# Cross-attention and gated expert attention on one core: turned x tiles by DMA, a reordered prologue, and the last batch's projection in pieces

## The chip, the core and the metric

One core of a Trainium2 chip runs the whole program. The metric is the device time of one launch in microseconds (us); lower is better.

## The reference, cut to what matters

`x` is 8 batches of 512 rows of 512 values, `ctx` 8 batches of 77 rows.

```python
x = x + (softmax(mask(layernorm(x) @ ctx.T * scale)) @ ctx).swap(-1, -2) @ W_merge.T + b_merge   # per batch
h = layernorm(x)                                                # taken as 4 x 1024 rows
rw = softmax(relu-gated cosine logits of h against sim, 16 experts)
q, k, v = [sum_e rw[e] * (h @ proj[e]) for proj in (q_proj, k_proj, v_proj)]    # head width 64
a = softmax(causal(q @ k.T / 8)) @ v
x = x + sum_e rw[e] * (a @ o_proj[e])
```

Gating and attention work on whole rows. Products are made in three parts of a high and a low half of each operand (`products`), so each expert product is 12 matmuls.

## The kernel before

Rows are taken in tiles of 128; a batch is 4 tiles. The program is written by hand for each engine: one instruction stream for TensorE (PE), VectorE (DVE), ScalarE (ACT), GpSimd (POOL) and SyncE (SP), joined by semaphores. Every engine works strictly in the order of its stream, and SP issues every DMA, all on one queue.

After a prologue, a batch is 32 slots, `k` from 0 to 31; slot `k` is expert pair `g = k % 8` of tile `j = k // 8`. In each slot TensorE makes 12 expert matmuls into one of four banks `psQ` (400 columns for `g` = 0, 384 otherwise). Around them the body places the other work of the kernel by slot, from tables at the head of the file:

- **Cross attention, five tiles ahead** (`X1_LEAD`). At `g` = 0 (`X1_T_SLOT`) TensorE turns the x tile in `H` with four transposes into `psT`, and ScalarE and VectorE copy it to the pair `hT` (`copy_rows`, `low_rows`). `x1_score` follows at `g` = 4, its softmax after it (`x1_limit`, `x1_exp`, `x1_invert`, `x1_high`, `x1_low`).
- **The next tile's h.** `sum_x2` and `add_x2` at `g` = 2, its row statistics, GpSimd's `powers`, `normalise` at `g` = 4, and at `g` = 6 four transposes of `H` (`move_rows`).
- **The causal attention of the batch**, from slot 15 on: turned q and k (`QK_T_AT`), scores into `psM` (`SCORES_AT`), reciprocal and scaling, turned probabilities (`PROBS_T_AT`), values into `psM` (`VALUES_AT`).
- **The output projection.** For each half of the batch (two tiles) and each of four groups `u` of experts: `MIX_AT` multiplies `spread` (the gates, repeated over partitions by a DMA) with the attention, `MIX_LO_AT` makes its low part, `PROJECT_AT` makes 12 matmuls of 512 columns, six into `psO` and six into `psM`. `Y_AT` adds the residual.

Slots over 31 in a table lie in the next batch. For the last batch there is no next one: slots 32 to 48 are a body without expert products.

The prologue takes the first five tiles through cross attention, makes the first merged matrix `G`, the normalised `sim`, the first h, and starts on the high and low parts of the expert weights (`w_high`, `w_low`, 8 pieces of 128x1536), which go on into the first slots. ScalarE and VectorE also make the parts of `w_o` in slots 9 to 23.

## Time and profile before

| | |
|---|---|
| median of 3 runs | 931.87 us (930.38 to 932.78) |
| profiled execution | 931.5 us, its span 929.8 us |
| busy: PE, weight loads, DVE, ACT, POOL | 894.8, 834.4, 646.0, 224.3, 126.0 us |
| mean granted TensorE clock | 0.982 |
| DMA | 88.60 MB, 95 GB/s over the span |

The profile has one execution's instructions with start and duration. Matmuls overlap, so their durations add up to more than the time; the distance between two starts tells what one costs. A bracket behind a row is the idle time of the engine before it, and who ended it.

### The profile page before, as it was taken

What the parts mean: (1) busy time and instruction counts of PE and PEld (TensorE: products, weight loads), DVE (VectorE), ACT (ScalarE), POOL (GpSimd) and SP (SyncE); (2) the same over time, 40 slices, a digit from 0 to 9 for tenths busy, and PEclk for the clock granted to TensorE, in tenths of its full rate; (3) what the DMA queues carried; (4) which work ended last, traced back from release to release, by engine and by line L of the source; (5) the groups of instructions that cost most, each with busy time, mean ns of one, the idle gap of its engine ahead of it and who ended that gap; (6) DMA issues with size and microseconds to landing.
All of it is one profiled execution on the core that took longest, in us unless ns stands there. A gap on an engine that the chain in (4) does not pass through costs nothing.

```text
span 929.8 us, 16166 instructions
## 1 busy us (share of the span) xinstructions
PE 894.8 (96%) x5000; PEld 834.4 (90%) x5000; DVE 646.0 (69%) x1964; ACT 224.3 (24%) x570; POOL 126.0 (14%) x333
## 2 busy tenths in 40 slices
PE   6679999999999999999999999999999999999976
PEld 5579999999999899999999999999999999999965
DVE  6788877767586776767777676776758676666643
ACT  4522312213131221212212131211312121121121
POOL 3221111201111110111111011110101211110100
PEclk9699999999999999999999999999999999999997
DMA  8912513144141531334113441414314251132131
GB/s 265 342 54 77 171 38 83 60 113 134 49 116 38 135 104 48 104 86 152 47 60 93 94 153 37 113 40 119 129 45 107 64 145 38 50 91 69 35 72 42
DMA packets 63493, 88.60 MB, mean 95 GB/s; under 512 B 10297, under 2 KB 33497, under 8 KB 63170
## 3 DMA queue, kind: packets, MB, share of 16 engines
q1 hardware_dynamic: 63426, 87.84, 32.3%
q8 instruction: 25, 0.41, 0.2%
q14 instruction: 42, 0.34, 0.1%
HBM read 68.68 MB, written 19.14 MB: 94 GB/s over the span
## 4 chain that ended last, share of the span: by engine, by line
PE 79%; DVE 7%; issue 6%; DMA 4%; SPq 1%; DVEq 1%; ACT 1%; POOLq 1%; POOL 1%; ACTq 0%
PE psQ L1212 47%; PE psO L1305 10%; PE psM L1305 9%; PE psT L1130 3%; DMA MASK<-in_mask 2%; PE psT L1162 2%; PE psO L1153 2%; PE psM L1280 2%; DMA merge_lo<-merge_scratch 1%; PE psT L1145 1%; DVE neg_mx L1043 1%; PE psT L1147 1%; DVE acc L919 1%; PE psT L1239 1%; PE psT L1220 1%
## 5 line engine op out<-in xcount | busy, mean ns | idle before, releaser
L1212 PE MATMUL psQ<-Wqkv_hi,hT_hi 128*128 128x384 f32 (+1 forms) x1024 | 352.6, 344 | 4.7 <-DVE hT_lo L795 2.9
L1212 PE MATMUL psQ<-Wqkv_lo,hT_hi 128*128 128x384 f32 (+1 forms) x1024 | 347.6, 339 | 0.0
L1212 PE MATMUL psQ<-Wqkv_hi,hT_lo 128*128 128x384 f32 (+1 forms) x1024 | 347.6, 339 | 0.0
L919 DVE SCALAR_TENSOR_TENSOR acc<-psQ,RW,acc 128x192 f32<-128x192 f32 x448 | 165.0, 411 | 130.9 <-PE psQ L1212 128.6
L1212 PEld LDWEIGHTS psQ<-Wqkv_hi,hT_hi 128*128 128x128 f32 x1024 | 193.3, 189 | 11.1 <-DVE hT_lo L795 3.3
L1212 PEld LDWEIGHTS psQ<-Wqkv_lo,hT_hi 128*128 128x128 f32 x1024 | 193.4, 189 | 4.7
L1212 PEld LDWEIGHTS psQ<-Wqkv_hi,hT_lo 128*128 128x128 f32 x1024 | 193.4, 189 | 0.0
L551 POOL TENSOR_TENSOR pow_tmp<-b_mv,eps 128x1 f32<-128x1 f32 x32 | 7.5, 234 | 682.0 <-DVE b_mv L872 682.0
L755 ACT ACTIVATE mixedT_hi<-spread 128x512 fp32r<-128x512 f32 x64 | 40.5, 632 | 203.6 <-DVE spread L1095 148.2
L619 ACT ACTIVATE hT_hi<-psT 128x512 fp32r<-128x512 f32 x64 | 38.0, 595 | 134.5 <-PE psT L1130 134.5
L1305 PE MATMUL psO<-Wo_hi,mixedT_hi 128*128 128x512 f32 x128 | 55.1, 431 | 2.7 <-DVE mixedT_lo L1086 2.7
L795 DVE TENSOR_TENSOR hT_lo<-psT,hT_hi 128x512 fp32r<-128x512 f32 x64 | 44.0, 688 | 15.3 <-ACT hT_hi L619 14.6
L1305 PE MATMUL psO<-Wo_hi,mixedT_lo 128*128 128x512 f32 x128 | 50.8, 397 | 0.0
L1305 PE MATMUL psO<-Wo_lo,mixedT_hi 128*128 128x512 f32 x128 | 50.6, 395 | 0.0
L1305 PE MATMUL psM<-Wo_lo,mixedT_hi 128*128 128x512 f32 x128 | 50.4, 394 | 0.0
L1305 PE MATMUL psM<-Wo_hi,mixedT_lo 128*128 128x512 f32 x128 | 50.4, 394 | 0.0
L1305 PE MATMUL psM<-Wo_hi,mixedT_hi 128*128 128x512 f32 x128 | 50.3, 393 | 0.0
L1086 DVE TENSOR_TENSOR mixedT_lo<-spread,mixedT_hi 128x512 fp32r<-128x512 f32 x64 | 43.5, 680 | 7.0 <-ACT mixedT_hi L755 6.0
L1095 DVE TENSOR_TENSOR spread<-spread,attT 128x512 f32<-128x512 f32 x64 | 43.5, 680 | 3.5 <-ACT attT L766 3.5
L738 ACT ACTIVATE qkT<-psT 128x256 fp32r<-128x256 f32 x32 | 12.3, 384 | 139.4 <-PE psT L1239 139.4
L1130 PE MATMUL psT<-ident,H 128*128 128x128 f32 x236 | 36.1, 276 | 3.9 <-DVE H L876 2.9
L881 DVE SCALAR_TENSOR_TENSOR logit<-psQ,pow_out,neg_sig 128x16 f32<-128x16 f32 x32 | 7.5, 234 | 43.8 <-PE psQ L1212 43.8
(178 smaller groups left out, 1283.5 us busy)
## 6 DMA issues: line engine op xcount, KB each, us to landing
spread<-gates_scratch SPq DMA_DIRECT2D x32, 512.0 KB, 6.6
X<-in_x SPq DMA_DIRECT2D x32, 256.0 KB, 2.7
x_scratch<-X SPq DMA_DIRECT2D x32, 256.0 KB, 2.0
resid<-x_scratch SPq DMA_DIRECT2D x32, 256.0 KB, 4.1
out<-resid SPq DMA_DIRECT2D x32, 256.0 KB, 2.4
merge_hi<-merge_scratch SPq DMA_DIRECT2D x28, 256.0 KB, 2.9
merge_lo<-merge_scratch SPq DMA_DIRECT2D x28, 256.0 KB, 3.3
H<-in_x SPq DMA_DIRECT2D x27, 256.0 KB, 2.9
```

The lines of the kernel that those rows point to most:

```text
L619: act.activation(hT[p][0][:], psT[moves.bank()][:], ACT.Copy).then_inc(moved_hi, 1)
L755: act.activation(mixedT[0][:, 2 * (u % 2):2 * (u % 2) + 2, :], spread[:, 2 * u:2 * u + 2, :], ACT.Copy).then_inc(mix_hi, 1)
L795: dve.tensor_tensor(dst, src, dst_hi.bitcast(F32), ALU.subtract).then_inc(moved_lo, 1)
L919: dve.scalar_tensor_tensor(out=acc[e][:], in0=src, scalar=w, in1=acc[e][:], op0=ALU.mult, op1=ALU.add).then_inc(expert_added, 1)
L1086: dve.tensor_tensor(mixedT[1][:, 2 * (u % 2):2 * (u % 2) + 2, :], spread[:, 2 * u:2 * u + 2, :], mixedT[0][:, 2 * (u % 2):2 * (u % 2) + 2, ...
L1095: dve.tensor_tensor(pair_of, pair_of, attT[:].unsqueeze(1).broadcast_to([P, 2, 2 * P]), ALU.mult).then_inc(mix_made, 1)
L1130: last = pe.transpose(bank[:, c * P:(c + 1) * P], tile[:, c * P:(c + 1) * P], ident[:])
L1153: last = pe.matmul(psO[0:CP, :], a[:, q, :], w, start=(q == 0 and n == 0), stop=(q == TILES - 1 and n == 2))
L1162: last = pe.matmul(bank[:], a[:], w[:], start=(n == 0), stop=(n == 2))
L1212: last = pe.matmul(psQ[g % 4][:, 0:first_col(g) + PW], a[:, c * P:(c + 1) * P], w[:, c, E + g * PW - first_col(g):E + (g + 1) * PW], start ...
L1280: last = pe.matmul(psM[:, cols], v[:, s, :, :].rearrange("p r d -> p (r d)"), w[:, s * 2 * P:s * 2 * P + cols.stop], start=(m == 0), stop= ...
L1305: last = pe.matmul((psO, psM)[i][:], a[:, 2 * (u % 2) + c, place(i)], w[:, 2 * u + c, :], start=(u == 0 and c == 0 and n == 0), stop=(u == ...
```

## The change

The host gives the kernel a second copy of x, `x_t`, in which each 128x512 tile is already turned.

1. **Turned tiles.** The four transposes at `g` = 0 go. SP loads the turned tile into `XT` at the tile's first slot (`load_xt`), ScalarE and VectorE make `hT` of it at `g` = 2 (`turned_high`, `turned_low`).
2. **Prologue.** ScalarE issues the first four turned tiles on its own DMA queue. The first two expert weight pieces are issued earlier, `w_o` in slots 5 and 11. The squares of `sim` and the bias' low part move to GpSimd, the 128x16 power there comes before the fifth tile. The fifth tile's scores and softmax move to slots 3 and 4. The low parts of weight pieces 0 and 1 are made in halves, between which the first h is worked on.
3. **Last batch.** Tiles 2 and 3 are turned at slots 26 and 32, scored at 28 and 33. The first half's projection is in pieces in slots 31 to 37, the second half's in 38 to 41, in banks of its own (`psQ` 2 and 3); the last scores and values use `psQ` 0 and 1. The gates of the last half come in four loads.

```diff
 QK_T_AT = ({15: 0, 18: 1, 31: 2, 34: 3},
-           {15: 0, 18: 1, 31: 2, 34: 3})
+           {15: 0, 18: 1, 26: 2, 32: 3})
 SCORES_AT = ({18: 0, 20: 1, 34: 2, 36: 3},
-             {18: 0, 20: 1, 34: 2, 36: 3})
+             {18: 0, 20: 1, 28: 2, 33: 3})
 INVERT_AT = ({19: 0, 21: 1, 35: 2, 37: 3},
-            {19: 0, 21: 1, 35: 2, 37: 3})
-PROBS_T_AT = ({21: 0, 23: 1, 37: 2, 39: 3},) * 2
-SCALE_AT = ({20: 0, 22: 1, 36: 2, 38: 3},) * 2
+            {19: 0, 21: 1, 29: 2, 34: 3})
...
 SPREAD_SLOT = 16
 SPREAD_1_SLOT = 3
-VALUES_AT = ({25: 0, 41: 1},) * 2
+LAST_SPREAD_AT = {31: (0, 1), 34: (2,), 36: (3,)}
+VALUES_AT = ({25: 0, 41: 1}, {25: 0, 35: 1})
 MIX_AT = ({26: (0, 0), 27: (0, 1), 28: (0, 2), 29: (0, 3),
            42: (1, 0), 43: (1, 1), 44: (1, 2), 45: (1, 3)},
-          {26: (0, 0), 27: (0, 1), 28: (0, 2), 29: (0, 3),
-           42: (1, 0), 43: (1, 1), 44: (1, 2), 45: (1, 3)})
+          {26: (0, 0), 27: (0, 1), 32: (0, 2), 34: (0, 3),
+            36: (1, 0), 37: (1, 1), 38: (1, 2), 39: (1, 3)})
 MIX_LO_AT = tuple({k + 1: job for k, job in at.items()} for at in MIX_AT)
-PROJECT_AT = tuple({k + 2: job + ((0, 1),) for k, job in at.items()} for at in MIX_AT)
+PROJECT_AT = ({k + 2: job + ((0, 1),) for k, job in MIX_AT[0].items()},
+              {31: (0, 0, (0,)), 32: (0, 0, (1,)), 33: (0, 1, (0, 1)), 34: (0, 2, (0,)), 35: (0, 2, (1,)),
+                36: (0, 3, (0,)), 37: (0, 3, (1,)), 38: (1, 0, (0, 1)), 39: (1, 1, (0, 1)), 40: (1, 2, (0, 1)),
+                41: (1, 3, (0, 1))})
+STORE_Y_AT = ({31: 0, 33: 1, 47: 2, 48: 3}, {38: 0, 39: 1, 47: 2, 48: 3})
 Y_AT = ({31: 0, 32: 1, 47: 2, 48: 3},
-        {31: 0, 32: 1, 47: 2, 48: 3})
+        {38: 0, 39: 1, 41: 2, 42: 3})
...
-X1_T_SLOT, X1_MOMENTS_SLOT, X1_SCORE_SLOT, X1_INV_SLOT, X1_LOW_SLOT = 0, 3, 4, 5, 6
+X1_HIGH_SLOT, X1_MOMENTS_SLOT, X1_SCORE_SLOT, X1_INV_SLOT, X1_LOW_SLOT = 2, 3, 4, 5, 6
...
+SCORE_4_SLOT, ATT_4_SLOT = 3, 4
 WO_AT = {9 + 2 * n: n for n in range(8)}
+WO_LOAD_AT = {5: 0, 11: 1}
+RESID_SLOT = 25
...
+        def project_banks(h, ab):
+
+            return (psQ[2], psQ[3]) if h == 1 and last_batch(ab) else (psO, psM)
...
+                def load_xt(t, p):
+
+                    if isinstance(t, int) and t == 0:
+                        sp.wait_ge(x1_max_ready, TILES)
+                    else:
+                        sp.wait_ge(qkv_summed, PAIRS * t)
+                    sp.dma_start(XT[p][:], turned(t + X1_LEAD)).then_inc(xt_in, 16)
...
+                load_w(0)
+                sp.dma_start(xt_first[TILES], turned(TILES)).then_inc(ld_xt[TILES], 16)
...
+                load_w(1)
...
+                        if cross and g == 0 and not (is_first(b) and j == 0):
+                            load_xt(t, (j + 1) % 2)
...
+                    if n == 1:
+                        pool.wait_ge(ld_sim, 16)
+                        pool.tensor_tensor(sim_sq, sim_f, sim_f, ALU.mult).then_inc(sim_squared, 1)
+                        pool.wait_ge(bias_made, 1)
+                        pool.tensor_tensor(bias_lo, bias_f, bias_hi.bitcast(F32), ALU.subtract).then_inc(bias_made, 1)
+                pool.wait_ge(sim_floored, 1)
+                pool.tensor_tensor(sim_rn, sim_ss, half_e, ALU.pow).then_inc(sim_rooted, 1)
...
+                act.dma_start(xt_first[0], turned(0)).then_inc(ld_xt[0], 16)
                 act.wait_ge(ld_ctx[0], 16)
                 centre(ctx_first[0], centre_dump, 0)
+                for n in range(1, TILES):
+                    act.dma_start(xt_first[n], turned(n)).then_inc(ld_xt[n], 16)
                 act.wait_ge(dve_init, 1)
                 copy_ctx()
-                copy_rows(0)
-                copy_rows(1)
+                turned_high(0, 0)
+                turned_high(1, 1)
                 act.wait_ge(ld_bias, 16)
...
+                def turned_low(t1, p):
+
+                    dve.wait_ge(xt_hi, t1 + 1)
+                    src = xt_first[t1] if isinstance(t1, int) and t1 < X1_LEAD else XT[p][:]
+                    high, low = x1_parts[t1] if isinstance(t1, int) and t1 < X1_LEAD else hT[p]
+                    dve.tensor_tensor(low[:, 0:D], src, high[:, 0:D].bitcast(F32), ALU.subtract).then_inc(xt_lo, 1)
...
+                    chunks = slice(0, KC) if half is None else slice(half * KC // 2, (half + 1) * KC // 2)
+                    last = dve.tensor_tensor(Wv[1][:, chunks, cols], W_raw[:, chunks, cols],
+                                             Wv[0][:, chunks, cols].bitcast(F32), ALU.subtract)
+                    if half != 0:
+                        last.then_inc(w_lo, 1)
...
-                G_low(0)
-                dve.wait_ge(gate_e_made, 1)
-                link(dve.tensor_scalar(gate_e, gate_e, 1.0, None, ALU.add))
-                link(dve.reciprocal(gate_e, gate_e))
-                dve.tensor_scalar(neg_sig[:], gate_e, -1.0, None, ALU.mult).then_inc(const_ready, 1)
-                x2_moved = add_x2(None)
-                dve.wait_ge(sim_summed, 1)
-                dve.tensor_scalar(sim_ss, psM[:, 0:E], NORM_FLOOR ** 2, None, ALU.max).then_inc(sim_floored, 1)
-                row_stats(x2_moved)
-                low_ctx()
-                w_low(0)
+                turned_low(TILES, 0)
...
                 last.then_inc(sim_normed, 1)
+                dve.wait_ge(gate_e_made, 1)
+                link(dve.tensor_scalar(gate_e, gate_e, 1.0, None, ALU.add))
+                link(dve.reciprocal(gate_e, gate_e))
+                link(dve.tensor_scalar(neg_sig[:], gate_e, -1.0, None, ALU.mult))
+                G_low(0)
+                w_low(0, 0)
+                x2_moved = add_x2(None)
+                row_stats(x2_moved)
+                dve.wait_ge(sim_hi, 1)
+                dve.tensor_tensor(simn[1], sim_f, simn[0].bitcast(F32), ALU.subtract).then_inc(sim_lo, 1)
+                w_low(0, 1)
+                normalise(0, 0)
+                low_ctx()
+                w_low(1, 0)
                 low_rows(0)
-                normalise(0, 0)
-                x1_limit(TILES, 0)
-                dve.wait_ge(sim_hi, 1)
-                dve.tensor_tensor(simn[1], sim_f, simn[0].bitcast(F32), ALU.subtract).then_inc(const_ready, 1)
-                w_low(1)
-                low_rows(0)
+                w_low(1, 1)
                 w_low(2)
-                x1_invert(TILES, 0)
-                x1_low(TILES, 0, 0)
...
-                        if cross and g == X1_T_SLOT:
-                            move_rows(H, x1_in, 32 * (t + 1))
-                            x1_moved = moves.now()
+                        if qkv and is_first(b) and k == SCORE_4_SLOT:
+                            x1_score(TILES, 0)
...
+                                if h == 0 and last_batch(ab):
+                                    pe.wait_ge(exp_done, TILES * ab + 3)
...
         "x": _np.asarray(x),
+        "x_t": _np.asarray(x).reshape(-1, 128, D // 128, 128).transpose(0, 3, 2, 1).reshape(-1, D),
```

TensorE in the middle of batch 0, first before, then after (`H` is the x tile, `psQ` takes the expert products):

```order
L1212 MATMUL psQ<-Wqkv_lo,hT_hi 128x400
L1212 MATMUL psQ<-Wqkv_hi,hT_lo 128x400
L1130 MATMUL psT<-ident,H 128x128 x4
L1212 MATMUL psQ<-Wqkv_hi,hT_hi 128x384
L1212 MATMUL psQ<-Wqkv_lo,hT_hi 128x384
```
```order
L1302 MATMUL psQ<-Wqkv_hi,hT_hi 128x400
L1302 MATMUL psQ<-Wqkv_lo,hT_hi 128x400
L1302 MATMUL psQ<-Wqkv_hi,hT_lo 128x400
L1302 MATMUL psQ<-Wqkv_hi,hT_hi 128x384
L1302 MATMUL psQ<-Wqkv_lo,hT_hi 128x384
```

The transposes between the 400-column and the 384-column products are gone.

VectorE in the prologue, before from the first x2 sum on, after from the low part of `G` on (`H` is the first normalised tile, the last `hT_lo` in each the turned form of a tile, `spread` the space in which `sim` is prepared):

```order
L865 TENSOR_TENSOR X<-psT,X 128x512
L972 TENSOR_SCALAR spread<-psM 128x16
L870 BN_STATS b_stats<-X 128x6
L872 BN_AGGR b_mv<-b_stats 128x2
L795 TENSOR_TENSOR ctxT<-psT,ctxT 128x2x77 x2
L848 TENSOR_TENSOR Wqkv_lo<-W_raw,Wqkv_hi 128x4x384
L978 TENSOR_TENSOR spread<-spread 128x16 x4
L795 TENSOR_TENSOR hT_lo<-psT,hT_hi 128x512
L876 TENSOR_SCALAR H<-X,b_mv,pow_out 128x512
L819 COPY sc<-psT 128x77
L821 TENSOR_TENSOR sc<-psT,sc 128x77
L825 SCALAR_TENSOR_TENSOR sc<-sc,x_scale,limit 128x77
```
```order
L951 TENSOR_TENSOR G_lo<-psO,G_hi 77x512
L939 TENSOR_TENSOR Wqkv_lo<-W_raw,Wqkv_hi 128x2x384
L958 TENSOR_TENSOR X<-psT,X 128x512
L963 BN_STATS b_stats<-X 128x6
L965 BN_AGGR b_mv<-b_stats 128x2
L1070 TENSOR_TENSOR Wqkv_lo<-spread,Wqkv_hi 128x4x16
L939 TENSOR_TENSOR Wqkv_lo<-W_raw,Wqkv_hi 128x2x384
L969 TENSOR_SCALAR H<-X,b_mv,pow_out 128x512
L878 TENSOR_TENSOR ctxT<-psT,ctxT 128x2x77 x2
L939 TENSOR_TENSOR Wqkv_lo<-W_raw,Wqkv_hi 128x2x384
L878 TENSOR_TENSOR hT_lo<-psT,hT_hi 128x512
L939 TENSOR_TENSOR Wqkv_lo<-W_raw,Wqkv_hi 128x2x384
```

Half of a weight piece stands where the wait for the sum is, the other half after the statistics; the first h no longer has a whole piece and the fifth tile's low part ahead of it, and its own `hT_lo` follows after half a piece.

TensorE after the last expert product, before:

```order
L1239 MATMUL psT<-ident,nat 128x128 x2
L1261 MATMUL psM<-qkT 128x384
L1262 MATMUL psM<-causal_r,ident_r 128x128
L1264 MATMUL psM<-kT_lo,qkT 128x384
L1261 MATMUL psM<-qkT 128x512
L1262 MATMUL psM<-causal_r,ident_r 128x128
L1264 MATMUL psM<-kT_lo,qkT 128x512
L1220 MATMUL psT<-ident,probs 128x128 x7
L1280 MATMUL psM<-probsT_hi,V_hi 128x256
```

After, around the last scores, and around the last turned probabilities:

```order
L1403 MATMUL psM<-Wo_lo,mixedT_hi 128x512
L1403 MATMUL psM<-Wo_hi,mixedT_lo 128x512
L1357 MATMUL psQ<-qkT 128x512
L1358 MATMUL psQ<-causal_r,ident_r 128x128
L1360 MATMUL psQ<-kT_lo,qkT 128x512
L1403 MATMUL psO<-Wo_hi,mixedT_hi 128x512
L1403 MATMUL psO<-Wo_lo,mixedT_hi 128x512
L1403 MATMUL psO<-Wo_hi,mixedT_lo 128x512
L1403 MATMUL psO<-Wo_hi,mixedT_hi 128x512
```
```order
L1403 MATMUL psM<-Wo_hi,mixedT_lo 128x512
L1310 MATMUL psT<-ident,probs 128x128 x4
L1403 MATMUL psO<-Wo_hi,mixedT_hi 128x512
L1403 MATMUL psO<-Wo_lo,mixedT_hi 128x512
L1403 MATMUL psO<-Wo_hi,mixedT_lo 128x512
L1403 MATMUL psO<-Wo_hi,mixedT_hi 128x512
L1403 MATMUL psO<-Wo_lo,mixedT_hi 128x512
L1403 MATMUL psO<-Wo_hi,mixedT_lo 128x512
L1376 MATMUL psQ<-probsT_hi,V_hi 128x256
```

Before, the whole chain of two softmaxes stands with nothing between its parts. After, one softmax is left here, and projection matmuls of the first half stand between its parts.

## Rows read from the trace of the kernel before

**Rows 1.** The page: busy time of each engine, TensorE's granted clock in 40 slices.
```profile
PE 894.8 (96%) x5000; PEld 834.4 (90%) x5000; DVE 646.0 (69%) x1964; ACT 224.3 (24%) x570; POOL 126.0 (14%) x333
...
PEclk9699999999999999999999999999999999999997
```

**Rows 2.** TensorE at a tile's first slot (start us, duration us; timeline).
```profile
308.82 0.60 PE L1130 MATMUL psT<-ident,H 128*128 128x128 f32 x4
309.17 0.42 PE L1212 MATMUL psQ<-Wqkv_hi,hT_hi 128*128 128x384 f32 x1
309.43 0.33 PE L1212 MATMUL psQ<-Wqkv_lo,hT_hi 128*128 128x384 f32 x1
309.60 0.34 PE L1212 MATMUL psQ<-Wqkv_hi,hT_lo 128*128 128x384 f32 x1
```

**Rows 3.** Waits of TensorE's weight loads, then DMA (us in total, times, longest us).
```profile
PEld psT L1130 <- DMA MASK<-in_mask: 2.1, 4, 0.7
```

**Rows 4.** DMA issues of the page (count, size, median us to landing).
```profile
spread<-gates_scratch SPq DMA_DIRECT2D x32, 512.0 KB, 6.6
...
H<-in_x SPq DMA_DIRECT2D x27, 256.0 KB, 2.9
```

**Rows 5.** VectorE in the prologue and the first slots (timeline).
```profile
29.69 0.17 DVE L972 TENSOR_SCALAR spread<-psM 128x16 f32<-128x16 f32 x1 [0.83 <-PE psM L1182]
...
30.54 0.18 DVE L872 BATCH_NORM_AGGREGATE b_mv<-b_stats 128x2 f32<-128x6 f32 x1
...
34.01 0.55 DVE L876 TENSOR_SCALAR H<-X,b_mv,pow_out 128x512 f32<-128x512 f32 x1
...
39.04 0.68 DVE L795 TENSOR_TENSOR hT_lo<-psT,hT_hi 128x512 fp32r<-128x512 f32 x1
...
57.59 1.73 DVE L848 TENSOR_TENSOR Wqkv_lo<-W_raw,Wqkv_hi 128x1536 fp32r<-128x1536 f32 x1
```

**Rows 6.** GpSimd in the same stretch (timeline).
```profile
29.94 2.92 POOL L583 TENSOR_TENSOR spread<-spread 128x16 f32<-128x16 f32 x1 [4.05 <-DVE spread L972]
32.82 0.19 POOL L551 TENSOR_TENSOR pow_tmp<-b_mv,eps 128x1 f32<-128x1 f32 x1
...
57.76 1.61 POOL L551 TENSOR_TENSOR pow_tmp<-b_mv,eps 128x1 f32<-128x1 f32 x1 [21.72 <-DVE b_mv L872]
```

**Rows 7.** TensorE around the first slots (timeline).
```profile
35.77 1.11 PE L1130 MATMUL psT<-ident,H 128*128 128x128 f32 x4
39.78 0.70 PE L1212 MATMUL psQ<-Wqkv_hi,hT_hi 128*128 128x400 f32 x1 [2.90 <-DVE hT_lo L795]
...
53.28 0.41 PE L1212 MATMUL psQ<-Wqkv_hi,hT_hi 128*128 128x384 f32 x1 [1.84 <-DVE acc L916]
...
65.18 0.63 PE L1130 MATMUL psT<-ident,H 128*128 128x128 f32 x4 [2.88 <-DVE H L876]
```

**Rows 8.** TensorE after the last batch's last expert product (timeline).
```profile
895.28 0.48 PE L1305 MATMUL psO<-Wo_hi,mixedT_hi 128*128 128x512 f32 x1
...
899.24 0.44 PE L1261 MATMUL psM<-qkT 128*128 128x384 f32 x1 [0.73 <-DVE resid L1038]
...
901.50 0.50 PE L1261 MATMUL psM<-qkT 128*128 128x512 f32 x1 [1.54 <-ACT probs L760]
...
905.22 1.09 PE L1220 MATMUL psT<-ident,probs 128*128 128x128 f32 x4 [2.25 <-ACT probs L713]
907.76 0.55 PE L1280 MATMUL psM<-probsT_hi,V_hi 128*128 128x256 f32 x1 [1.46 <-issue]
...
913.41 0.76 PE L1305 MATMUL psO<-Wo_hi,mixedT_hi 128*128 128x512 f32 x1 [2.75 <-DVE mixedT_lo L1086]
...
925.90 0.39 PE L1305 MATMUL psM<-Wo_lo,mixedT_hi 128*128 128x512 f32 x1
926.13 0.39 PE L1305 MATMUL psM<-Wo_hi,mixedT_lo 128*128 128x512 f32 x1
```

**Rows 9.** The page's costliest groups: ScalarE's copy of a turned tile.
```profile
L619 ACT ACTIVATE hT_hi<-psT 128x512 fp32r<-128x512 f32 x64 | 38.0, 595 | 134.5 <-PE psT L1130 134.5
```

224 lines of the change are left out of this document (134 added, 90 removed).

## The prediction

> **What bounds the kernel now.** I began with the page [rows 1]. TensorE is busy for 96% of the span and its granted clock reads 9 tenths or more in all slices but two, the second (6) and the last (7), so what is not TensorE at full pace must lie near the start and near the end. The other engines are far below: VectorE 69%, ScalarE 24%. The waits of TensorE by releaser then say the same: between the first slots and the end of the last expert product they are a microsecond or two in all, the largest group of them being the transposes of the x tile, whose weight loads wait 2.1 us in 4 places for the tile's DMA [rows 3]. So three stages have to be read apart. In the middle, an instruction taken off TensorE is time taken off the kernel. In the prologue, TensorE starts on the first expert product at 39.78 us and waits for VectorE three times around the first slots: 2.90, 1.84 and 2.88 us [rows 7]. At the end, it waits five times after the last expert product, 0.73, 1.54, 2.25, 1.46 and 2.75 us, together 8.73 us, along a chain of scores, softmax, values and mixing that has no other work beside it [rows 8].
>
> **The middle: the transposes go.** Four transposes stand from 308.82 to 309.17, 0.35 us by starts. The product behind them takes 0.26 us to the next start instead of 0.17, another 0.08. That is 0.43 us for a tile [rows 2]. The loads of `H` count 27 such tiles [rows 4]. The first lies in the opening slots, which I count with the prologue, so 26 x 0.43 = 11.2 us. The 2.1 us of waits for the tile's DMA [rows 3] go as well, if the turned tile comes in time: its load is issued at the tile's first slot, such a load lands in 2.9 us [rows 4], and it is wanted two slots later, over 4 us, by ScalarE, and by TensorE only four slots later. But 27 more loads of 256 KB share the DMA engines with the `spread` and `merge` loads, for which TensorE has a few short waits too; I let half of the 2.1 us come back and take 1.1. ScalarE and VectorE make the same two copies as before, 0.60 and 0.68 us, from SBUF instead of PSUM [rows 5, 9]. Middle: **12.3 us**, bounds 9 and 13.3.
>
> **The prologue.** Removed are the transposes of five tiles, from the path of the scores to the first `G`. VectorE still has one tile's moments, low part, limits and attention in each round, so its round of about 3.2 us a tile stays; the first scores come about 1.3 us earlier, since `hT` no longer waits for PSUM, and the bias' low part goes off VectorE. But `G`'s low part now stands behind the fifth tile's low part, the four scalings of `sim` and the gates' reciprocals, about 1.8 us that VectorE did later before. So I put the first x2 sum where it was. From there:
> - Statistics. Before, the mean was made at 30.54, after 0.83 us of waiting for the sum of squares [rows 5]. That wait is gone: 29.7 us.
> - GpSimd. Before, it was in the 128x16 power from 29.94 to 32.86 and began the first h's powers only at 32.82; from there to the `H` at 34.01 are 1.19 us [rows 5, 6]. Now the power is made in the shadow of the last merge parts. But half a weight piece, 1.73 / 2 = 0.87 us, starts on VectorE as the statistics end, and the rows show what that does: GpSimd's first small add takes 0.19 us at 32.82, with no weight piece on VectorE, and 1.61 us at 57.76, ending at 59.37, just as the 1.73 us weight piece that began at 57.59 ends [rows 5, 6]. So I let GpSimd start at 30.6: `H` begins at 31.8 and ends at 32.3, against 34.56. Gain 2.3 us.
> - Behind `H`. Before, from 34.56 to the first product at 39.78 were 5.2 us, since TensorE had the fifth tile's scores first and the low part waited behind a whole weight piece [rows 5, 7]. Now: transposes 1.11, ScalarE 0.60, VectorE 0.68 and some 0.2 of handovers, 2.6 us [rows 5, 7, 9]. Gain 2.6 us. The first product starts at 34.9.
> - Slots 0 to 6. VectorE owes all that it owed, and now also the fifth tile's limits and low part, about 1.5 us, in slots 3 and 4; the low parts of weight pieces 1 to 7, the gates and the sums follow one another without a break, so the wait at slot 4 stays about 1 us and the one at slot 6 grows to some 3.5. TensorE's new scores in slot 3 lie in the first of these waits. What is left at slot 6, at 65.18 before [rows 7], I put at 5.0 us.
>
> The second DMA queue and the earlier weights cost nothing on the path and give nothing of their own. Prologue: **5.0 us**. Bounds: 1.5, if all that VectorE saves is owed again by slot 6, and 7, if the earlier scores also bring `G` forward.
>
> The Trainium skill, page "SBUF — State Buffer", section "Who interferes with whom", says that a VectorE instruction with two SBUF inputs and a GpSimd instruction that reads SBUF exclude each other. By that rule, the trace agrees at 57.76 us. It speaks against this change, since the new low part of a turned tile has two SBUF inputs where the old one read PSUM; rival 5 prices that.
>
> **The end.** Before, from 895.28 us to the end of the span at 929.8 were 34.5 us. The projection of a group is 12 matmuls at 0.23 us [rows 8], 2.75 us. Of eight groups, three lay before that point and now lie behind; the scores and probabilities of tile 2 (0.2 of transposes, 0.75 and 0.5 us) now lie before it. The point itself moves from 895.3 forward by 3 x 2.75 - 1.4 = 6.9 us. Behind it TensorE now has 8 x 2.75 = 22.0 us of projection, turned q and k 0.2, scores 0.8, turned probabilities 0.6 and values. The values took 2.90 us, the 5.65 us between the two rows less the wait of 2.75; at the full clock half, 1.45. Sum 25.1. Is all of it covered? Scores to transposes took 3.7 us [rows 8]; the 0.8 of the scores and a group of 2.75 fill 3.55. Transposes to values took 2.54, of which some 0.4 by the clock; the transposes and half a group fill 2.0. Values to the first mixed group took 5.65, by the clock 4.2; the values and three half groups fill 5.6. I allow 0.5 us for handovers. From the last matmul to the end are 3.7 us by starts, 3.3 by its end, as before [rows 8]. So the end has 25.1 + 0.5 + 3.3 = 28.9 us behind a point 6.9 us earlier: 34.5 - 28.9 + 6.9 = 12.5. The same from the other side: waits of 8.7, and what the half clock cost the values (1.45), the transposes (0.5) and the first ten projections of 0.43 instead of 0.23 us (2.0), 12.6. I take **12.2 us**. Bounds 6 and 12.6: the low one if the mixed groups of the second half, which need spread loads of 6.6 us at the median [rows 4], come late.
>
> **Sum.** 12.3 + 5.0 + 12.2 = 29.5 us. The profiled execution took 931.5 us, 1.7 over its span and 0.4 under the median of 931.87; it gives 902.0 us.
>
> **Rivals.**
> 1. *More comes.* All waits go, `G` comes forward: 7 + 13.3 + 12.6, 898.6 us. Against it: VectorE is in every round of the prologue. Chance 0.14.
> 2. *The prologue gives it back.* VectorE's debt of weight pieces and the fifth tile decides slot 6. For it: a weight piece takes VectorE 1.73 us [rows 5], and seven of the eight are still to be made. Prologue 1 us, 906.0. Chance 0.16.
> 3. *The end has new waits.* ScalarE's mixed high parts and VectorE's low parts stand in strict order behind the softmax's. End 6 us, 908.2. Chance 0.10.
> 4. *Turned tiles come late,* and TensorE waits about as long as it transposed. For it: SP is one queue, and the load stands behind its wait for the last product. Middle 0: 914.3. Chance 0.03.
> 5. *GpSimd is held up by the low part's second SBUF input in every tile,* and so the next h: up to 0.68 us in 27 tiles, 18 us, 920. Against it: the low part stands ahead of the statistics for which GpSimd waits. Chance 0.02.
> 6. *Nothing is left,* the waits only move: 931. Chance 0.01.
> 7. *Slower.* The load of a turned tile at the head of SP's stream holds back what stands behind it, the x2 tile, statistics stores and `merge`. It decides from 29.5 / 26 = 1.1 us a tile; at 2 us it is 902 + 52 = 954. Against it: SP is idle at a tile's start. Chance 0.02.
>
> The forecast itself has 0.52, its own range 899.5 to 904.5.
>
> **The numbers.** The range of 80% takes in the forecast, most of rivals 1 and 2 and some of 3: 897 to 908.5. A change of 0.3% is about what a measurement can tell from none. Faster by more: rivals 1 to 5 and the forecast, 0.97; same 0.01; slower 0.02.
>
> **What would show it.** After: tiles a distance of 0.4 us or more shorter in the middle, with no `H` transposes behind 400-column products; the first product near 34.9 us; the `H` transposes of slot 6 near 60; a granted clock that stays full from there to the end; 29 us from the end of the last expert product to the end of the span. Wrong would be: TensorE waiting for `hT_lo` or `XT` at `g` = 4; waits over 1 us between the last groups; slot 6 at 63 us or later.

## The result: 906.5 us, and the profile after

The changed kernel takes 906.5 us (median of 4 runs, 905.3 to 908.5), the kernel before 931.1 us in the runs beside it. The ratio is 0.9737, with a 95% interval of 0.9712 to 0.9761: 24.6 us faster. The prediction was 902.0 us with a range of 897 to 908.5, so the time lies inside it, 4.5 us above the point. The profiled execution took 906.4 us with a span of 904.7.

The page of the changed kernel answers [rows 1]: TensorE has 128 matmul records fewer, and the last slice's clock, 7 before, is 9.

```profile
PE 873.0 (96%) x4872; PEld 815.1 (90%) x4872; DVE 642.6 (71%) x1964; ACT 226.3 (25%) x570; POOL 129.1 (14%) x335
...
PEclk9799999999999999999999999999999999999999
```

I cut both traces at the same three places: the start of the first expert product, the start of the second tile's first product (tile 1), and that of the last tile.

| | before | after | gain | predicted |
|---|---|---|---|---|
| first product starts (part of the next line) | 39.78 | 37.44 | 2.3 | 4.9 |
| tile 1 starts | 67.8 | 65.4 | 2.4 | 5.0 |
| tile 1 to the last tile | 801.2 | 791.5 | 9.7 | 12.3 |
| last tile to the end of the span | 60.8 | 47.8 | 13.0 | 12.2 |
| sum | | | 25.1 | 29.5 |

**The end** (timeline of TensorE; answers [rows 8]). The first row is the last matmul of the last expert product, and the fourth tile's scores, its turned probabilities and the values follow with projections between them. No row has a wait behind it, and the values start at 0.11 to 0.20 us a matmul where they stood at the lower clock before. From the last product to the end of the span are 904.7 - 875.5 = 29.2 us; 28.9 were predicted.

```profile
875.50 0.34 PE L1302 MATMUL psQ<-Wqkv_hi,hT_lo 128*128 128x384 f32 x1
877.36 0.41 PE L1328 MATMUL psT<-ident,nat 128*128 128x128 f32 x2
879.00 0.40 PE L1357 MATMUL psQ<-qkT 128*128 128x512 f32 x1
...
882.57 0.63 PE L1310 MATMUL psT<-ident,probs 128*128 128x128 f32 x4
884.66 0.36 PE L1376 MATMUL psQ<-probsT_hi,V_hi 128*128 128x256 f32 x1
884.86 0.28 PE L1376 MATMUL psQ<-probsT_lo,V_hi 128*128 128x256 f32 x1
...
900.99 0.40 PE L1403 MATMUL psQ<-Wo_hi,mixedT_lo 128*128 128x512 f32 x1
```

**The middle** (timeline of TensorE at a tile's first slot; answers [rows 2]). The 400-column product is followed directly by the 384-column one, 0.18 us from start to start, with no transposes between.

```profile
303.21 0.35 PE L1302 MATMUL psQ<-Wqkv_hi,hT_lo 128*128 128x400 f32 x1
303.39 0.34 PE L1302 MATMUL psQ<-Wqkv_hi,hT_hi 128*128 128x384 f32 x1
```

Tile by tile, the distance between starts falls from 31.53 to 31.06 us and from 21.30 to 20.90 us, as predicted. Only the third tile of a batch does not follow: its eight distances sum to 187.3 us before and 188.0 after, where 7 x 0.43 = 3.0 us should have come off. TensorE's waits from 85 to 860 us (in total, times, longest) show most of why; before, the same stretch had 1.7 us for merge in 3 places, none of them at the second sum of `G`.

```profile
PE psO L1250 <- DMA merge_lo<-merge_scratch: 4.6, 7, 1.7
PE psO L1403 <- DVE mixedT_lo L1179: 0.2, 1, 0.2
```

That is 2.9 of the 3.7 us by which the third tiles miss the forecast; for the rest no run has a cause. There is one wait for merge to a batch, in five batches at the second sum of `G`, in slot 19 (4.0 us in all), and in two at the third, in slot 21. The longest is at a second sum. By the rows of SP's queue and TensorE its merge load is issued behind the turned tile and the megabyte of `spread`, and the sum waits for it until 204.59.

```profile
192.21 0.43 SPq L461 DMA_DIRECT2D XT<-in_x_t  x1
192.74 1.28 SPq L484 DMA_DIRECT2D spread<-gates_scratch  x2
...
197.46 0.33 SPq L467 DMA_DIRECT2D merge_hi<-merge_scratch  x1
197.83 0.43 SPq L467 DMA_DIRECT2D merge_lo<-merge_scratch  x1
```
```profile
204.59 0.42 PE L1250 MATMUL psO<-merge_hi,att_hi 128*78 128x512 f32 x1 [1.73 <-DMA merge_lo<-merge_scratch]
```

The tile's first product starts at 192.28 here, so `spread` is issued 0.5 us behind that start. Before, the same tile starts at 197.45 and `spread` is issued 5.7 us ahead of it, as in all batches from the second on (rows of SP's queue, before):

```profile
191.73 1.28 SPq L440 DMA_DIRECT2D spread<-gates_scratch  x2
196.99 0.35 SPq L448 DMA_DIRECT2D out<-resid  x1
203.05 0.33 SPq L423 DMA_DIRECT2D merge_hi<-merge_scratch  x1
```

Two parts of the change stand ahead of `spread` in SP's stream now. One is the turned tile's load with its wait for the last product. The other is easily overlooked: `STORE_Y_AT` stores the third and fourth result tile of a batch in slots 15 and 16, not in 16 and 17 as before. The first of these stores waits for its tile until 191.82 and used to stand behind the spread loads.

**The prologue** (timelines of ScalarE, VectorE and GpSimd; answer [rows 5, 6]). ScalarE waits 4.11 us for turned tile 1, which ScalarE itself had issued at 4.60 us; VectorE then waits 2.96 us for ScalarE.

```profile
11.18 0.63 ACT L695 ACTIVATE hT_hi<-XT 128x512 fp32r<-128x512 f32 x1 [4.11 <-DMA XT<-in_x_t]
```
```profile
11.84 0.69 DVE L888 TENSOR_TENSOR hT_lo<-XT,hT_hi 128x512 fp32r<-128x512 f32 x1 [2.96 <-ACT hT_hi L695]
...
28.66 0.69 DVE L951 TENSOR_TENSOR G_lo<-psO,G_hi 77x512 fp32r<-77x512 f32 x1 [0.84 <-ACT G_hi L722]
...
31.90 0.18 DVE L965 BATCH_NORM_AGGREGATE b_mv<-b_stats 128x2 f32<-128x6 f32 x1
...
34.09 0.55 DVE L969 TENSOR_SCALAR H<-X,b_mv,pow_out 128x512 f32<-128x512 f32 x1 [1.02 <-POOL pow_out L613]
```
```profile
32.16 0.95 POOL L610 TENSOR_TENSOR pow_tmp<-b_mv,eps 128x1 f32<-128x1 f32 x1 [3.91 <-DVE b_mv L965]
```

The first `x_max`, the end of the first scores, is made at 13.83 us instead of 12.04, `G`'s low part at 28.66 instead of 25.75, the mean at 31.90 instead of the 29.7 that I had put. From there on the steps are those of the prediction: GpSimd's first add takes 0.95 us beside half a weight piece, and from the end of `H` to the first product are 2.8 us (predicted 2.6). TensorE around the first slots (answers [rows 7]):

```profile
37.44 0.70 PE L1302 MATMUL psQ<-Wqkv_hi,hT_hi 128*128 128x400 f32 x1 [1.41 <-DVE hT_lo L878]
...
62.81 0.64 PE L1226 MATMUL psT<-ident,H 128*128 128x128 f32 x4 [1.90 <-DVE H L969]
...
65.38 0.34 PE L1302 MATMUL psQ<-Wqkv_hi,hT_hi 128*128 128x400 f32 x1
```

### The profile page after: what moved, and what is told of

Read it like the earlier page. It is cut to its first block, busy times and chain, and to the rows that moved or that the text cites. A ratio compares the mean times of both kernels' runs of the same rounds, so it can differ in the third digit from the quotient of the medians.

```text
span 904.7 us, 15909 instructions
## 1 busy us (share of the span) xinstructions
PE 873.0 (96%) x4872; PEld 815.1 (90%) x4872; DVE 642.6 (71%) x1964; ACT 226.3 (25%) x570; POOL 129.1 (14%) x335
## 4 chain that ended last, share of the span: by engine, by line
issue 65%; PE 19%; POOLq 9%; POOL 3%; DMA 2%; DVE 1%; DVEq 0%; ACT 0%; SPq 0%
PE psQ L1302 11%; PE psM L1403 2%; POOLq L615 2%; PE psO L1403 2%; POOLq L595 2%; POOLq L618 2%; PE psQ L1403 1%; POOL limit L598 1%; POOLq L612 1%; POOLq L597 1%; POOLq L620 1%; DMA XT<-in_x_t 1%; POOL pow_out L621 1%; POOL pow_tmp L611 1%; DMA merge_lo<-merge_scratch 1%
## 5 line engine op out<-in xcount | busy, mean ns | idle before, releaser
L1403 PE MATMUL psO<-Wo_hi,mixedT_hi 128*128 128x512 f32 x120 | 51.6, 430 | 0.2 <-DVE mixedT_lo L1179 0.2
L1403 PE MATMUL psO<-Wo_hi,mixedT_lo 128*128 128x512 f32 x120 | 47.3, 394 | 0.0
L1403 PE MATMUL psM<-Wo_hi,mixedT_lo 128*128 128x512 f32 x120 | 47.1, 392 | 0.0
L1403 PE MATMUL psM<-Wo_lo,mixedT_hi 128*128 128x512 f32 x120 | 47.1, 392 | 0.0
L1403 PE MATMUL psO<-Wo_lo,mixedT_hi 128*128 128x512 f32 x120 | 47.0, 392 | 0.0
L1403 PE MATMUL psM<-Wo_hi,mixedT_hi 128*128 128x512 f32 x120 | 47.0, 392 | 0.0
L817 ACT ACTIVATE qkT<-psT 128x256 fp32r<-128x256 f32 x32 | 12.3, 384 | 125.4 <-PE psT L1328 125.4
L1242 PE MATMUL psT<-ctxT,hT_hi 128*128 128x156 f32 x124 | 31.6, 323 | 9.0 <-DVE hT_lo L888 7.2
L848 ACT ACTIVATE gate_exp<-logit,gate_bias 128x16 f32<-128x16 f32 x32 | 9.9, 308 | 117.0 <-DVE gate_bias L981 117.0
L1242 PEld LDWEIGHTS psT<-ctxT,hT_hi 128*128 128x128 f32 x124 | 25.8, 208 | 9.8 <-issue 5.9
```

Of the source, the lines that this page charges most:

```text
L817: act.activation(qkT[:, :, i * P:(i + 1) * P], src, ACT.Copy).then_inc(moved_hi, 1)
L848: act.activation(gate_exp[:], logit[:], ACT.Exp, bias=gate_bias[:, 0:1]).then_inc(gate_exp_ready, 1)
L1242: pe.matmul(bank[:, 0:2 * CP], high, ctxT[:, c, :, :].rearrange("p a k -> p (a k)"), start=(c == 0), stop=False, skip_group_check=True)
L1403: last = pe.matmul(project_banks(h, ab)[i][:], a[:, 2 * (u % 2) + c, place(i)], w[:, 2 * u + c, :], start=(u == 0 and c == 0 and n == 0), ...
```

## The experiments

Twelve kernels ran. All ratios are to the kernel before on the same chip; the changed kernel's own is 0.9737.

**1. The end alone undone.** The last batch's tables, banks and waits are those of before; the loads of `spread` and of the residual follow them.

```diff
-           {15: 0, 18: 1, 26: 2, 32: 3})
+           {15: 0, 18: 1, 31: 2, 34: 3})
...
-          {26: (0, 0), 27: (0, 1), 32: (0, 2), 34: (0, 3),
-            36: (1, 0), 37: (1, 1), 38: (1, 2), 39: (1, 3)})
+          {26: (0, 0), 27: (0, 1), 28: (0, 2), 29: (0, 3),
+           42: (1, 0), 43: (1, 1), 44: (1, 2), 45: (1, 3)})
...
-            return isinstance(ab, int) and ab == B - 1
+            return False
```

> The changed kernel with the last batch's tables, banks and waits as in the kernel before; prologue and turned tiles as changed. Theory (the end is worth 13.0 us by itself, as the two traces give it from the last tile's start): 906.5 + 13 = 919.5 us, about 60.5 us from the last tile's start to the end of the span, and the waits behind the last expert product back at 8 to 9 us. Rival (part of the 13 us comes from the turned tiles or from the clock of an earlier stage): 912 to 916 us, and a distance well under 60.

Measured: 922.0 us, ratio 0.989 (0.9868 to 0.9912). From the last tile's start to the end of the span are 920.9 - 859.2 = 61.7 us, against 47.8: 13.9 us. The five waits are back (timeline of TensorE), and so is the lower clock behind the values:

```profile
889.37 0.44 PE L1354 MATMUL psM<-qkT 128*128 128x384 f32 x1 [0.73 <-DVE resid L1126]
...
891.64 0.50 PE L1354 MATMUL psM<-qkT 128*128 128x512 f32 x1 [1.54 <-ACT probs L836]
...
895.34 1.09 PE L1307 MATMUL psT<-ident,probs 128*128 128x128 f32 x4 [1.89 <-ACT probs L789]
897.89 0.55 PE L1373 MATMUL psM<-probsT_hi,V_hi 128*128 128x256 f32 x1 [1.46 <-issue]
...
903.54 0.76 PE L1400 MATMUL psO<-Wo_hi,mixedT_hi 128*128 128x512 f32 x1 [2.75 <-DVE mixedT_lo L1176]
904.10 0.63 PE L1400 MATMUL psO<-Wo_lo,mixedT_hi 128*128 128x512 f32 x1
```

The end's gain stands by itself; the rival that some of it belongs to the turned tiles falls. The time is 2.5 us above the expected 919.5: the six runs lie between 916.8 and 923.3 us, and in the profiled one the middle took 795.3 us instead of 791.5 and the end 0.9 us more than in the kernel before.

**2. How much of the end is the clock.** Experiment 1 with 27 added matmuls in four of its waits.

```diff
+FILL = {4: 5, 7: 7, 9: 5, 12: 10}
...
+                        if isinstance(b, int) and b == B and k in FILL:
+                            pe.wait_ge(expert_added, 2 * SLOTS * B)
+                            for _ in range(FILL[k]):
+                                pe.matmul(psQ[1][:], hT[0][0][:, 0:P], Wv[0][:, 0, E:E + 512], start=True, stop=True)
```

> The changed kernel with the last batch's tables of before (as in the first variant, 922.0 us), and 27 more matmuls of 512 columns, whose result nobody reads, in four of TensorE's waits behind the last expert product: 5 ahead of the fourth tile's scores, 7 ahead of its turned probabilities, 5 ahead of the values, 10 ahead of the second half's projection. It adds work and leaves none out, and moves none of the kernel's own. Theory (of the 12 to 13 us at the end, 3.9 are the lower clock in values, transposes and the first ten projections, and 8.7 are waits): with TensorE kept busy the clock stays at its upper level, the values' matmuls come at 0.11 to 0.12 us instead of 0.22, the projections at 0.23 from the first, the span ends 3.5 to 4 us earlier than in that variant, 918 us, and the rest of the gain stays with the moved projections. Rival A (the whole gain is the waits, the clock's part is small): 920.5 to 922. Rival B (the added matmuls outlast the waits): 922 or more.

Measured: 917.0 us, ratio 0.9849 (0.9826 to 0.9872). From the last expert product to the end: 915.3 - 884.05 = 31.2 us, against 920.9 - 885.09 = 35.8 in experiment 1. So 4.6 us come back with none of the kernel's own work moved; the theory said 3.5 to 4. The rows (timeline of TensorE): the values now step by 0.11 us where experiment 1 has 0.22, and the second half's projection steps by 0.23 us from its second matmul where that has 0.43.

```profile
896.60 0.28 PE L1378 MATMUL psM<-probsT_lo,V_hi 128*128 128x256 f32 x1
896.71 0.22 PE L1378 MATMUL psM<-probsT_hi,V_hi 128*128 128x128 f32 x1
...
901.08 0.39 PE L1405 MATMUL psO<-Wo_lo,mixedT_hi 128*128 128x512 f32 x1
901.31 0.39 PE L1405 MATMUL psO<-Wo_hi,mixedT_lo 128*128 128x512 f32 x1
```

Against the kernel before itself, whose end took 60.8 us, the same distance is 57.1, so 3.7 us. About 30% of the end's 13 to 14 us is thus the clock that waiting had cost, and the rest are the waits themselves.

**3. Turned tile 1 first.** Is the late landing a matter of one late issue?

```diff
-                act.dma_start(xt_first[0], turned(0)).then_inc(ld_xt[0], 16)
+                for n in range(2):
+                    act.dma_start(xt_first[n], turned(n)).then_inc(ld_xt[n], 16)
...
-                for n in range(1, TILES):
+                for n in range(2, TILES):
```

> The changed kernel, but ScalarE issues the load of turned tile 1 right behind that of tile 0, at about 1.2 us, ahead of the centring, instead of at 4.6. Theory (the prologue lost 2 to 3 us because turned tile 1 landed at 11.1 us behind what SP had issued first): it lands near 8, VectorE's wait of 2.96 us at 11.84 goes, the first x_max is written near 11.3 instead of 13.8, G's low part near 26.2 instead of 28.7, the first product starts near 35 and tile 1 near 63.0 instead of 65.4; 904.1 us. Rival A (VectorE's debt of weight pieces decides): the first product comes earlier, tile 1 still starts at 65.4, 906.5. Rival B (the DMA engines' total is what is late, not its order): another tile lands late instead, first product 37, 906.

Measured: 905.6 us, ratio 0.9725 (0.9709 to 0.9741). First product 35.80, tile 1 at 63.7: two thirds of the expected gain over the profile after, but hardly ahead of the earliest execution with the changed prologue (35.99, experiment 1). ScalarE no longer waits for turned tile 1, but the plain tile 0 now lands late, so that VectorE's first statistics begin at 6.14 instead of 5.25 us: rival B in part. And a cost showed in full that the profile after has in part (0.60 us at 13.15), in rows of VectorE and GpSimd of this kernel: the bias' low part, which the change moved to GpSimd, now ran at the moment of VectorE's limits, and an instruction of 0.30 us there took 1.29.

```profile
11.16 1.29 DVE L916 SCALAR_TENSOR_TENSOR sc<-sc,x_scale,limit 128x77 f32<-128x77 f32 x1 [0.16 <-issue]
```
```profile
11.10 1.25 POOL L641 TENSOR_TENSOR merge_lo<-spare_wo,kT_lo 1x512 fp32r<-1x512 f32 x1
```

**4. One queue.** SP issues each turned tile behind its plain tile, ScalarE none.

```diff
                     sp.dma_start(x_first[n], row(x, n)).then_inc(ld_x[n], 16)
+                    sp.dma_start(xt_first[n], turned(n)).then_inc(ld_xt[n], 16)
...
-                act.dma_start(xt_first[0], turned(0)).then_inc(ld_xt[0], 16)
...
-                for n in range(1, TILES):
-                    act.dma_start(xt_first[n], turned(n)).then_inc(ld_xt[n], 16)
```

> The changed kernel, but the turned tiles of the prologue are issued by SP, each right behind its x tile, and ScalarE issues none. Theory (what counts is how many bytes are issued ahead of turned tile 1, not the number of queues): turned tile 1 is issued near 3.9 us with 0.9 MB ahead of it and before tiles 2, 3 and merge, lands at 8 to 9; the first product near 35.5, 904.5 us; the second queue has no value. Rival (the second queue is what makes the changed prologue 2.4 us faster than before's): the first product at 38 or later, 908 us.

Measured: 906.0 us, ratio 0.9717 (0.9698 to 0.9737). Turned tile 1 is used at 7.60 us, the first product starts at 33.13, earlier than in any other kernel here. But tile 1 starts at 63.5: of the 4.3 us won over the profile after 1.9 are left, and the time is that of the changed kernel within what can be told. (The profiled execution took 907.8 us, the longest of five from 903.4 to 907.8, so the others may have lost less.) TensorE waits 3.48 us instead of 1.90 at slot 6, and behind that wait product 6 runs at the lower clock, 0.32 us a matmul for 12 matmuls instead of 0.175 (timeline of ScalarE, then TensorE):

```profile
7.60 0.63 ACT L696 ACTIVATE hT_hi<-XT 128x512 fp32r<-128x512 f32 x1 [1.25 <-DMA XT<-in_x_t]
```
```profile
33.13 0.70 PE L1300 MATMUL psQ<-Wqkv_hi,hT_hi 128*128 128x400 f32 x1 [1.41 <-DVE hT_lo L876]
...
59.33 0.64 PE L1224 MATMUL psT<-ident,H 128*128 128x128 f32 x4 [3.48 <-DVE H L967]
...
60.31 0.52 PE L1300 MATMUL psQ<-Wqkv_hi,hT_lo 128*128 128x384 f32 x1
60.63 0.52 PE L1300 MATMUL psQ<-Wqkv_hi,hT_hi 128*128 128x384 f32 x1
```

The late start is thus a matter of what is issued, where and behind what: this run changes the queue and the order together, and with them the arrangement of two queues is shown to cost, not to give; experiment 3, which changed the order alone, only moved the wait to another tile. The Trainium skill, page "DMA: Bandwidth & Descriptors", section "Issuing engines are not separate DMA queues", says that DMAs issued from SP and ScalarE run on the same 16 DMA engines. By that rule a second queue brings no bandwidth. This run does not contradict it: with nothing on the second queue, turned tile 1 is used 3.6 us earlier, though its issue is 1.4 us earlier too (3.19 against 4.60).

**5. The half weight piece away from GpSimd's powers.**

```diff
-                w_low(0, 1)
                 normalise(0, 0)
                 low_ctx()
-                w_low(1, 0)
+                w_low(0, 1)
                 low_rows(0)
+                w_low(1, 0)
                 w_low(1, 1)
```

> The changed kernel, but VectorE makes the second half of weight piece 0 behind the normalisation, under the H transposes, instead of beside GpSimd's powers. Theory (GpSimd's first small add is held while that subtraction runs, 0.95 us instead of 0.19): from the end of the statistics (the b_mv row) to the H row 1.5 us instead of 2.19, VectorE waits some 1.3 us for pow_out instead of 1.02 but has nothing else to do, the first product 0.7 us nearer to b_mv; tile 1 then moves by 0 to -0.7, since the half piece is still owed: 906.0 us. Rival (the add is slow at its first use whatever VectorE does): 2.1 us or more from b_mv to H, first product no nearer, 906.5.

Measured: 906.3 us, ratio 0.973 (0.9706 to 0.9753). GpSimd's first add takes 0.19 us again, and from `b_mv` (31.43) to `H` are 1.43 us instead of 2.19:

```profile
31.70 0.19 POOL L610 TENSOR_TENSOR pow_tmp<-b_mv,eps 128x1 f32<-128x1 f32 x1 [3.79 <-DVE b_mv L965]
```
```profile
32.86 0.55 DVE L969 TENSOR_SCALAR H<-X,b_mv,pow_out 128x512 f32<-128x512 f32 x1 [1.14 <-POOL pow_out L613]
```

The exclusion is real and worth 0.76 us there. It is owed back: from the first product to tile 1 are 28.8 us instead of 27.9.

**6. Weight piece 5 ahead of the gates' exponential**, on top of experiment 4.

```diff
-                        if qkv and is_first(b) and k + 4 < PAIRS:
-                            w_high(k + 4)
+                        if qkv and is_first(b) and k + 5 < PAIRS:
+                            if k == 0:
+                                w_high(4)
+                            w_high(k + 5)
```

> The variant with one queue, and ScalarE makes the high part of weight piece 5 ahead of the gates' exponential instead of behind it. Theory (in slots 0 to 6 VectorE is what the first H transposes of slot 6 wait for, so each idle microsecond of it there counts one for one): its wait of 1.36 us at 42.39 goes, the H transposes of slot 6 come near 58.0 instead of 59.33, tile 1 near 62.0 to 62.4 instead of 63.5; 904.8 us. Rival (VectorE waits again at the next thing, or TensorE's lower clock takes it): tile 1 at 63.2 or later, 906.

Measured: 903.2 us, ratio 0.9698 (0.9674 to 0.9721). VectorE's wait of 1.36 us is gone. From the first product to slot 6's H transposes are 58.53 - 34.44 = 24.1 us; they are 26.2 in experiment 4 and 25.4 in both the kernel before and the changed one. The first product was later than in experiment 4 (34.4 against 33.1), so tile 1 came at 62.7. This edit has no part in it: it touches slot 0 and later, and the low part of `G` is 1.4 us later already (25.65 against 24.29). A good half microsecond of the 1.3 is again an instruction of VectorE beside the bias' low part on GpSimd, 1.25 us where experiment 4 has 0.67 (VectorE, then GpSimd); experiments 7 and 11, which have this start too, show the same:

```profile
11.76 1.25 DVE L888 TENSOR_TENSOR hT_lo<-probs,hT_hi 128x512 fp32r<-128x512 f32 x1
```
```profile
11.21 1.25 POOL L642 TENSOR_TENSOR merge_lo<-spare_wo,kT_lo 1x512 fp32r<-1x512 f32 x1
```

In experiment 4 that GpSimd subtraction ran at 10.41, 0.8 us earlier, and held nothing up. The four executions with one queue (experiments 4, 6, 7 and 11) start the first product between 33.1 and 34.5, 33.9 in the mean.

**7. Twelve added matmuls in slot 6's wait**, on top of experiment 4.

```diff
+                        if is_first(b) and k == H_T_SLOT:
+                            for _ in range(12):
+                                pe.matmul(psM[:], hT[0][0][:, 0:P], Wv[0][:, 0, E:E + 512], start=True, stop=True)
```

> The variant with one queue, with 12 more matmuls of 512 columns in slot 6 ahead of the H transposes, whose result nobody reads, in the 3.5 us in which TensorE waits for H. It adds work and leaves none out. Theory (after that wait the granted clock was at its lower level for the 12 matmuls of product 6, 0.32 instead of 0.175 us each, 1.6 us): with TensorE busy the product runs at 0.175 from its start, and tile 1 starts near 62.0 instead of 63.5; 904.4 us. Rival A (the lower clock there does not come from the wait but from what lay before it): the product stays at 0.32, tile 1 at 63.5 or later. Rival B: the added matmuls run at the lower clock themselves and outlast the wait, tile 1 at 64 or later, 907.

Measured: 905.1 us, ratio 0.9721 (0.9697 to 0.9745). Product 6 runs at 0.175 us a matmul and tile 1 starts at 61.8, 2.6 us behind the H transposes instead of 4.1. But this is not proof: in experiment 12, the changed kernel once more, the same wait was 3.47 us and no matmul behind it was slow. Three executions with a 3.5 us wait and nothing in it had 8 to 12 slow matmuls behind it (experiments 4, 6 and 10), one had none, and the two with added matmuls (7 and 11) had none.

**8. The turned tile behind the merge loads**, in the third tile of each batch.

```diff
-                        if cross and g == 0 and not (is_first(b) and j == 0):
+                        if cross and g == 0 and j != 2 and not (is_first(b) and j == 0):
...
+                        if cross and k == 17:
+                            load_xt(t, (j + 1) % 2)
```

> The changed kernel, but in the third tile of each batch SP issues the turned tile's load one slot later, behind the merge loads instead of ahead of the spread loads. Theory (TensorE's 4.6 us of waits for merge, against 1.7 before, are the turned tile's 256 KB in the queue ahead of spread and merge): the waits at the second sum of G fall back to 1.5 to 2 us in all, 903.6 us, and no wait for the turned tile appears. Rival A (the spread's megabyte alone makes the merge late): the waits stay at 4 us or more, 906. Rival B: ScalarE now waits for the turned tile and hands it on, 907 to 910.

Measured: 926.7 us, ratio 0.9949 (0.9931 to 0.9968): 20 us slower than the changed kernel, where the worst rival, B, had 0.5 to 3.5. Its mechanism is what happened, and went further. TensorE's waits for merge grow to 20.6 us. The rows of one batch, on four engines, are a chain. `XT`, issued last, lands behind everything; ScalarE waits for it, VectorE behind ScalarE has the x2 statistics still to make, SP waits for them before it stores the x2 tile, and the third merge load stands behind that store. The wait shows under the name of merge, on TensorE, 9 us after ScalarE's wait for `XT` and with VectorE and SP between them (rows of SP's queue, then ScalarE, VectorE, TensorE):

```profile
200.74 0.43 SPq L461 DMA_DIRECT2D XT<-in_x_t  x1
209.72 0.34 SPq L442 DMA_DIRECT2D x_scratch<-X  x1
...
211.32 0.43 SPq L467 DMA_DIRECT2D merge_lo<-merge_scratch  x1
```
```profile
206.04 0.63 ACT L697 ACTIVATE hT_hi<-XT 128x512 fp32r<-128x512 f32 x1 [7.95 <-DMA XT<-in_x_t]
```
```profile
206.71 0.69 DVE L890 TENSOR_TENSOR hT_lo<-XT,hT_hi 128x512 fp32r<-128x512 f32 x1 [3.05 <-ACT hT_hi L697]
```
```profile
215.11 0.64 PE L1252 MATMUL psO<-merge_hi,att_hi 128*78 128x512 f32 x1 [3.17 <-DMA merge_lo<-merge_scratch]
```

The total thus says nothing of my theory on the turned tile: the run added a worse cause than it took away. But the 20.6 us are 19.7 at the third sum and 0.9 at the second. At the second, of which the theory speaks, the waits fell from 4.0 us to 0.9 with the turned tile behind the merge loads (`spread` was also issued 0.5 us earlier by it).

**9. The spread loads in slot 22**: `SPREAD_SLOT = 16` becomes 22.

> The changed kernel with the spread loads of the first half issued in slot 22 instead of 16, behind two of the three merge loads that the next sum of G waits for; their first user is in slot 26. Theory (TensorE's 4.6 to 6.7 us of waits for merge in the changed kernel and its variants come from a merge load that queues behind the turned tile and a megabyte of spread): the waits at the second sum of G fall to below 0.5 us in all, no new wait at slots 26 to 29, 901.5 to 902.5 us. Rival A (merge is late because SP itself issues it late, behind its wait for the statistics): the waits stay at 4 us or more, 906. Rival B (the spread comes late for the mixing in slot 26): VectorE waits for spread and TensorE for the mixed groups, 908 or more.

Measured: 909.9 us, ratio 0.9774 (0.9752 to 0.9796). Both happened: the waits for merge fell to 2.6 us, none of them at the second sum, which rival A excludes, and rival B came in full, 6.8 us for mixed groups (waits of TensorE, 85 to 860 us):

```profile
PE psO L1403 <- DVE mixedT_lo L1179: 6.8, 6, 2.3
PE psO L1250 <- DMA merge_lo<-merge_scratch: 2.6, 6, 0.6
```

**10. The spread loads in slot 15**: `SPREAD_SLOT = 16` becomes 15.

> The changed kernel with the spread loads of the first half issued in slot 15 instead of 16, so ahead of the turned tile's load and half a tile's slot further ahead of the merge loads; slot 15 is the first in which the spread tile is free. Theory (the merge load of the second sum of G queues behind what was issued in slots 16 and 17): TensorE's waits for merge fall from 4.6 to 6.9 us to 2 us or less, nobody waits for spread, 903.5 us. Rival (the spread's loads now hold back the turned tile, as in the variant that issued it behind merge): ScalarE waits for XT, VectorE behind it, SP's third merge load comes late, 908 or more.

Measured: 905.5 us, ratio 0.9722 (0.9703 to 0.9743). The waits for merge are 3.6 us, the third tile's distances sum to 187.2, the middle is 790.9 us. The turned tile is not late. `spread` is issued 5.6 us ahead of the tile's first product again, as in the kernel before, since in slot 15 it stands ahead of the store. The waits at the second sum are all but gone, 0.3 us in the first batch and none after it, as the theory has it. The rest, 3.3 us where I had said 2 or less in all, stands at the third sum, as do nearly all of experiment 9's, and the queue ahead of that load is not what makes it late: in the changed kernel SP issues it at 423.06 in one batch, only when it is past the store of the x2 tile, for a sum at 427. That is the rival A of experiment 9, true for this sum. The 1 us that the medians differ is less than they can tell.

**11. Four edits together**: experiments 4, 6 and 10, and 7 with 14 matmuls.

> The changed kernel with four edits together: the turned tiles of the prologue on SP's queue, weight piece 5 made ahead of the gates' exponential, 14 matmuls whose result nobody reads in TensorE's wait of slot 6, and the spread loads of the first half in slot 15. Theory (each works in a place of its own): first product at 33 to 34.5 us, slot 6's H transposes near 58.5, tile 1 at 61 with product 6 at 0.175 us a matmul (62.7 without the added ones), 790.9 us from tile 1 to the last tile, 47.8 to the end of the span: a span of about 899.5, 901.3 us. Rival (the spread's earlier loads or VectorE's debts take it back): 903 to 905.

Measured: 901.2 us, ratio 0.9683 (0.9665 to 0.9702), below the changed kernel's interval: it beats both kernels. First product 34.5, tile 1 at 61.1, middle 790.2, end 47.8 us.

**12. The changed kernel once more**, unedited.

> The changed kernel once more, unedited, beside the variant above on the same chip. Theory (the prologue's start depends on when turned tile 1 lands, 10.4 to 11.2 us in the four executions with this prologue, and the waits for merge on how the loads of slots 15 to 17 fall, 4.6 to 6.9 us): first product between 36.0 and 37.5, middle between 791 and 796, 905.5 to 908 us. Rival (the executions differ only by the edits of each variant): first product 37.4 and middle 791.5 again.

Measured: 906.0 us, ratio 0.9741 (0.972 to 0.9761). First product 36.27, middle 791.9, waits for merge 4.6 us. The seven executions with the changed prologue (the changed kernel, experiments 1, 2, 8 to 10 and 12) used turned tile 1 between 10.4 and 11.2 us and started the first product between 36.0 and 37.4; the earliest has 10.38 and 35.99, the latest, which is the profile after, 11.18 and 37.44. Their mean first product is at 36.7, a gain of 3.1 us and not 2.3 over the one execution of the kernel before.

## Why the prediction came out as it did

The sum was 4.4 us too large: 2.6 us too much for the prologue, 2.6 for the middle, and 0.8 too little for the end. The transposes and the end worked as forecast; the steps that failed are the prologue's start and the loads' place in SP's queue. By its own steps:

- **"That is 0.43 us for a tile"**: right, 0.47 and 0.40 by the distances of the tiles that wait for nothing.
- **"I let half of the 2.1 us come back and take 1.1"**: this term was mis-sized, and twice. First, the 2.1 us are idle time of the weight loads, which run ahead of the matmuls. By the starts of the matmuls the four waits cost 1.3 us (0.49, 0.40, 0.68 and 0.49 us from the matmul ahead to the transposes instead of 0.18). Second, the loads are late elsewhere. `MASK` and `XT` are waited for no more, but the waits for merge went from 1.7 to 4.6 us, and to 4.6 to 6.9 in the other executions with `spread` in slot 16 and turned tiles at their place. With both, 11.2 + 1.3 - 2.9 = 9.6 us, and the middle measured 9.7 instead of 12.3. Bandwidth had been counted, the place in the queue had not: a turned tile and a megabyte of spread stand right ahead of the merge load of the second sum, which is wanted 4.9 us after its issue (5.5 and 10.4 us behind the tile's start in experiment 10). The waits at that sum were none before, 4.0 to 6.3 us in the nine executions with both ahead of it, 0.9 with the turned tile moved behind (experiment 8), and 0.3 and none with `spread` moved away (experiments 10 and 9). So it takes both. That `spread` stands there needs no turned tile: the earlier store holds it back too, since in experiment 8 it is issued at most 0.3 us behind and never more than 1.2 us ahead of the tile's start, not 5.6 ahead. The prediction has neither wait.
- **"The first scores come about 1.3 us earlier"** and **"the second DMA queue and the earlier weights cost nothing on the path"**: this failed, and with it "so I put the first x2 sum where it was". VectorE's first statistics began at 5.25 us instead of 4.13 (4.34 with one queue), turned tile 1 was used at 11.18, the first `x_max` came 1.8 us later than before, and `G` 2.9 later. With the tiles in one queue the scores are as early as I had put them (`x_max` at 10.25 to 10.5, the expected 10.7), and the first product comes at 33.1 to 34.5, ahead of my 34.9. Which part of that is the queue and which the order of the issues is not shown.
- **"I let GpSimd start at 30.6"**: from the mean to `H` I had 2.1 us, the trace has 2.19; experiment 5 shows the cause by taking it away.
- **"Behind H ... 2.6 us"**: 2.8. Right.
- **"What is left at slot 6 ... I put at 5.0 us"**: the debts are what they were, 25.4 us from the first product to slot 6's transposes in both kernels. So what is lost at the first product is lost at tile 1: slot 6's transposes start at 62.81, and I had them near 60. That VectorE's debt sets this stretch was rival 2's reason; experiment 6 takes 1.3 us out of it by letting ScalarE work ahead.
- **"The second half ... behind it 25.1"**: right, 29.2 us against 28.9, and 13.0 against 12.2 for the end. Its two halves, waits of 8.7 and clock of 3.9, were measured as 13.9 - 4.6 = 9.3 and 4.6 in experiments 1 and 2.
- The rivals: 2 (906.0 us) is nearest to the time, and that is luck. It leaves the prologue 1 us where 2.4 were measured, by a debt that stayed the same, and has nothing of the middle's loss. 7 names the middle's mechanism, a load at the head of SP's stream that holds back merge, but in every tile; it came at one sum of a batch. 4, a late turned tile, did not happen, yet experiment 8 shows how near it was: one slot later, and 20 us are gone. 5 did not happen in the loop. 1, 3 and 6 did not come.

## What to carry to other kernels

When work moves from an engine to a load, cost the load by its place in the queue: what is issued ahead of it, and which load with a near deadline now stands behind it. In a stream that works in order, a store moved by one slot brings its wait along; here it alone keeps `spread` 5 to 6 us later than before (experiment 8). A wait is named after the load that came last, not after the one that made it late; follow the issuing queue back to what it waited for itself. At the end of a kernel, independent matmuls kept back for the waits pay twice, for the wait and for the clock behind it.

## What the runs showed of the hardware

- GpSimd holds up VectorE as well as the reverse: a VectorE instruction with SBUF inputs took 1.29 us instead of 0.30 beside a GpSimd subtraction of 1.25 us on a single partition (experiment 3), another 1.25 instead of 0.67 (experiment 6).
- TensorE's granted clock fell to its lower level or held behind a wait of the same length, 3.46 to 3.48 us, in executions whose code is the same from that wait on (experiments 4, 6, 10 and 12). In the profile after it fell earlier, from 55.8 to 59.0 us, where the following wait hid it.
- Where four loads of 256 KB at the start are issued, on SP's queue between the others or on ScalarE's, makes 2.7 us at the first product (mean of four executions 33.9, of seven 36.7); a single pair of profiles, 33.1 and 37.4, would have said 4.3.
